# Four moves in program order in a fused transformer and expert kernel: DMA issue order, a GpSimd step, an activation table load and three VectorE instructions

## The reference

```
x = x + attn_block(layernorm(x))       # 4 layers, each:
    h = h + attention(ln(h))           #   16 heads of 8, causal mask, relative positions
    h = h + gelu(ln(h) @ W1.T + b1) @ W2.T + b2      # 128 -> 512 -> 128
x = x + experts(layernorm(x))
    shared = silu(x @ sg.T) * (x @ su.T) @ sd.T      # hidden size 256
    scores = sigmoid(x @ router.T)                   # 16 experts in 4 groups
    # the best 2 groups by their best two biased scores, then the best 4 experts of these;
    # weights = the chosen scores over their sum
    routed = sum of weight * (silu(x @ gate) * (x @ up)) @ down   # hidden size 32 each
```

## Time and profile before

| | |
|---|---|
| time, median of 3 runs | 2348.01 us (2346.59 to 2349.03) |
| the profiled execution | 2349.03 us |
| its span, first to last instruction | 2347.0 us |
| mean granted TensorE clock | 0.992 of full speed |
| PE busy | 2273.5 us, 97% |
| PE weight loads busy | 1971.6 us, 84% |
| DVE busy | 1995.8 us, 85% |
| ACT busy | 1838.7 us, 78% |
| POOL busy | 1142.6 us, 49% |

### The profile page before, as it was taken

The page is one execution under the profiler, slowest core; times in us unless marked ns, Lnnn a source line. Parts: engine busy times, 40 slices in busy tenths (PEclk is TensorE's granted clock), DMA queues, the critical chain, the costliest instruction groups (busy, mean ns, idle before and its releaser), DMA issues. The chain is left out here.

```text
span 2347.0 us, 83100 instructions
## 1 busy us (share of the span) xinstructions
PE 2273.5 (97%) x31360; PEld 1971.6 (84%) x31360; DVE 1995.8 (85%) x4943; ACT 1838.7 (78%) x2869; POOL 1142.6 (49%) x2089
## 2 busy tenths in 40 slices
PE   4999999999999999999999999999999999799999
PEld 3788888888888888888888888888888888678787
DVE  6899999988888888888888888888888887577775
ACT  2688888888888888888888888888888888655564
POOL 4555555555545554545554455554455544333332
PEclk8999999999999999999999999999999999899999
DMA  4444433333333333333333333333333332011100
GB/s 136 111 117 108 111 94 88 88 92 87 94 92 94 85 90 91 94 93 86 87 90 96 94 90 86 91 87 94 93 103 90 89 92 61 21 28 28 28 24 19
DMA packets 227431, 196.04 MB, mean 84 GB/s; under 512 B 29024, under 2 KB 225760, under 8 KB 227040
## 3 DMA queue, kind: packets, MB, share of 16 engines
q1 hardware_dynamic: 227040, 190.73, 30.2%
HBM read 14.46 MB, written 4.19 MB: 8 GB/s over the span
## 5 line engine op out<-in xcount | busy, mean ns | idle before, releaser
L995 DVE TENSOR_REDUCE rowmax<-bank 128x4 f32<-128x1024 f32 (+1 forms) x768 | 916.1, 1220 | 106.4 <-PE bank L572 73.9
L813 ACT ACTIVATE probs<-bank 128x1024 f32<-128x1024 f32 x768 | 737.7, 1024 | 82.3 <-PE bank L632 81.8
L632 PE MATMUL bank<-qstack,kstack 64*128 64x128 f32 (+1 forms) x4096 | 422.8, 299 | 4.2 <-DMA qstack<-maxrows 4.2
L572 PE MATMUL bank<-kstack,qstack 62*128 62x256 f32 (+1 forms) x4096 | 416.3, 300 | 9.5 <-DMA qstack<-base 9.5
L854 ACT ACT_TABLE_LOAD x256 | 328.4, 1283 | 4.5
L572 PEld LDWEIGHTS bank<-kstack,qstack 62*128 62x128 f32 x4096 | 315.7, 192 | 9.9 <-issue 9.9
L632 PEld LDWEIGHTS bank<-qstack,kstack 64*128 64x128 f32 x4096 | 315.1, 191 | 5.4 <-DMA qstack<-maxrows 5.4
L1169 POOL CAST xn1T_parts<-xn1T 128x256 fp32r<-128x256 f32 x128 | 50.7, 396 | 481.4 <-ACT xn1T L821 481.4
L594 PE MATMUL bank<-maskT_half,pick_half 64*128 64x128 bf16 (+1 forms) x3072 | 267.8, 241 | 10.9 <-DVE turn_c L964 2.6
L721 PE MATMUL bank<-w,hidden 128*128 128x128 f32 x2048 | 271.4, 276 | 2.7 <-ACT hidden L863 2.7
L652 PE MATMUL bank<-probs,v_pad 128*32 128x256 f32 x4096 | 271.1, 382 | 0.6 <-DVE v_tok L976 0.6
(11 more groups left out here) (153 smaller groups left out, 5187.4 us busy)
## 6 DMA issues: line engine op xcount, KB each, us to landing
qstack<-base SPq DMA_DIRECT2D x768, 128.0 KB, 2.5
kstack<-base SPq DMA_DIRECT2D x384, 128.0 KB, 2.5
turn_x<-turn_c SPq DMA_DIRECT2D x512, 32.0 KB, 1.9
qstack<-maxrows SPq DMA_DIRECT2D x256, 16.0 KB
out<-ot SPq DMA_DIRECT2D x16, 256.0 KB, 2.4
h_all<-in_x SPq DMA_DIRECT2D x7, 512.0 KB, 4.1
xin<-in_x SPq DMA_DIRECT2D x14, 256.0 KB, 3.2
w<-in_w SPq DMA_DIRECT2D x8, 256.0 KB, 3.1
```

The lines of the kernel that those rows point to most:

```text
L572: last = pe.matmul(bank[:, b0 + b, i * wide:(i + 1) * wide], qstack[rows, r, p0 + i, t * 128:(t + 1) * 128], kstack[rows, r, p0 + i, 0:wid ...
L632: last = pe.matmul(bank[:, b0 + b, i * wide:(i + 1) * wide], kstack[rows, r, p0 + i, kt * 128:(kt + 1) * 128], qstack[rows, r, p0 + i, q0: ...
L813: act.activation(probs[:, k], bank[:, A_BANK[k]:A_BANK[k] + 2, :], ACT.Exp, scale=SCALE).then_inc(exp_done[k], 1)
L995: dve.tensor_reduce(rowmax[:, n % 2, t, :, p0:p0 + heads], bank[:, M_BANK[k]:M_BANK[k] + 2, :].rearrange("p b (h c) -> p b h c", h=heads), ...
```

## The change

Four pieces of code are put elsewhere in their engine's program. No instruction is added or taken away.

- SP, layers: `content` of an item is issued at the head of the next slot, and so behind `exchange` of the same item and in front of its `turned_content`.
- POOL, layers: `turned(s)` is done at the end of slot s, behind `xn1_split(s+1)`, in place of in slot s+1 behind `xn2_split`. `split_qkv` then comes behind it.
- ACT, experts: the load of the Silu table comes directly behind the sigmoid, in front of the second `half_out`.
- DVE, experts: `weights_of_experts` is joined to the end of `routing_experts`, and so comes at u == 0 in place of u == 1 behind `result`.

```diff
@@ SP, layers
             for s in SLOTS:
                 if live(s - 1):
+                    content(s - 1)
+                if live(s - 1):
                     turned_content(s - 1)
                 if live(s - 3):
                     maxima(s - 3)
-                if live(s):
-                    content(s)
                 if live(s):
                     exchange(s)
@@ POOL, layers
                 if live(s - 6):
                     xn2_split(s - 6)
-                if live(s - 1):
-                    turned(s - 1)
...
                 if live(s + 1):
                     xn1_split(s + 1)
+                if live(s):
+                    turned(s)
@@ ACT, experts
                         act.activation(score[:].rearrange("p t e -> p (t e)"), bank[:, 6, 0:GT * E], ACT.Sigmoid
                                        ).then_inc(score_ready, 1)
+                        load_table(2 * (q + 1) + 1, ACT.Silu)
...
                     if live_tile(n - 2):
                         half_out(n - 2, 1)
-                    if u == 1 and live(q + 1):
-                        load_table(2 * (q + 1) + 1, ACT.Silu)
@@ DVE, experts
                 assert step[0] == ROUTE, step[0]
-
-            def weights_of_experts(q, v):
                 dve.tensor_scalar(wsum1[:], wsum[:], 1e-20, None, ALU.add).then_inc(route_end, 1)
...
-                    if u == 1 and live(q):
-                        weights_of_experts(q, v)
```

## The result

| | before | after |
|---|---|---|
| median (lowest to highest, runs) | 2347.66 us (2346.59 to 2349.03, 4) | 2381.52 us (2377.61 to 2389.59, 4) |
| ratio, 95% interval | | 1.0150 (1.0126 to 1.0175) |
| the profiled execution, its span | 2349.03, 2347.0 us | 2385.99, 2384.0 us |
| mean granted TensorE clock | 0.992 | 0.989 |

The forecast was 2360.2 us with a range to 2367. The profiled executions are 37.0 us apart, the medians 33.9.

A forecast was written before the change was run, and what follows sets the result against it. PE was taken to bound layers and experts, with a DMA chain pacing the first slots. Terms +5.7 - 4.2 - 2.2 + 12.9 = +12.2 us gave 2361.2 profiled, 2360.2 us against the median, range 2350 to 2367.

The forecast's parts named there:

- The sign: Whole kernel: the change makes it 0.5% slower; slower was given a chance of 0.86.
- the table load: Experts, ACT at u == 1: copy of hT and down product start 0.92 us later, 14 times, +12.9 us.
- A third sentence: Layers and experts: every engine other than PE has hundreds of microseconds free in both.
- The one-off loads: Layers, SP: loads behind an exchange, half a microsecond of issue each, fit into content's 2.9 us of cover; no cost.
- weights_of_experts: Experts, DVE: three small instructions moved before result(n-3) are hidden in 1.02 us of DVE idle time; 0 us.
- The six waits of the up product: Layers, slots with weight splits: PE waits for xn2_split behind turned, 3 x 0.58 + 3 x 1.33 = +5.7 us.
- The maxima: Layers, SP: maxima comes earlier, so PE's six waits for it go, -4.2 us, with 0 as other end.
- The first slots: Start of the layers: earlier exchange and turned_content(0) shorten PE's wait, -2.2 us, bounded by 0 and 6.7 us gained.
- The layers' three terms together: Layers: up product waits +5.7, maxima -4.2 and first slots -2.2 leave -0.7 us.
- rivals of a hidden: Experts: down does not wait for the later copy, experts cost 0, total 2347.3 us; chance 0.06.
- dearer switch: Experts: ACT empties itself before the table load, 17.9 us more, total 2378 us; chance 0.01.
- The cover of turn_x: Layers: turn_x lands 3.3 us, in some slots 1.4 us, before POOL ends xn1_split, so turned does not block POOL.

The follow-up runs named there:

- e10: The whole change, with the one-off loads issued from ACT's DMA queue in place of SP's; 2365.16 us, ratio 1.0077 against the kernel before.
- e4: Kernel before with only weights_of_experts moved, and POOL's exT_parts subtraction put behind its hw product; 2347.26 us against 2348.44, ratio 0.9994.
- e3: Kernel before with only weights_of_experts moved to the end of routing_experts; 2355.71 us, ratio 1.0028.
- e2: Kernel before with only the Silu table load moved directly behind the sigmoid; 2361.45 us, ratio 1.0056.
- e6: Kernel before with only POOL's turned moved to the end of its slot, exchange still behind content; 2423.96 us, ratio 1.0327.
- e12: The whole change, with the one-off loads issued by ACT one step later in its program, beside content; 2368.53 us against 2348.49 for the kernel before.

## Why the prediction was wrong

The sign, the table load and most of the layers' steps were right. Two steps were wrong, and both are sentences that put a cost at nothing. A third sentence is wrong without a part in the sum: the other engines do not have hundreds of microseconds free in the experts. DVE has 81 of 287 there and ACT 125.

**The one-off loads: the step that failed.** "The one-off loads behind an exchange, half a microsecond of issue each, fit into the same cover." I counted only the time in which SP issues them. But they are up to 512 KB each, and content now goes out while they move. It landed 5.4 and 7.6 us after its last issue where the prediction had 2.0, with 2.9 us of cover. The cost is the difference between the whole change and e10, where the same loads leave some 4 us ahead of content: 2381.5 - 2365.2 = 16.3 us. In the traces it is 13.8 us at the start (104.20 - 90.36), the slower clock behind the waits included, and 4.6 in slots 8 to 17 and 113: 18.4 in all, since the profiled execution of the changed kernel lies 4.5 us above its median.

**weights_of_experts: 0 in place of 7.1 us.** "DVE idles 1.02 us there for PE's down product, which hides them." The three instructions are as short as that on DVE alone (0.17, 0.18 and 0.22 us in e4). At their new place POOL's subtraction runs, and it stretches one of them from 0.17 to 1.12 us, which uses up the cover. e3 shows the cost, e4 that it goes when POOL is elsewhere.

**What held.**

- The six waits of the up product: 5.7 us forecast, 5.8 found in the lengths of the slots.
- The maxima: the wait is gone, as the 4.2 us had it. The slots that were longer before give back 3.0 us between f2(6) and f2(127), the rest lies in the start.
- The first slots: -2.2 us forecast. The times of the first round came within 0.4 us, and without loads beside content (e10) the start gained 4.4 us against the kernel before, slots 2 to 5 and their maxima included. Against e2, e3 and e4, with the same layers as before, it is 6.3 to 9.3, so the way is sure and the size is not.
- The layers' three terms together: -0.7 us forecast, and in e10, where the loads don't disturb them, -1.65 by f2(127) and -1.4 where the experts begin. The medians agree: 17.9 us for e10, less 12.4 and 7.1 for the experts, is -1.6. That near -0.7 is partly luck, since both the gain at the start and the six waits against it are several microseconds.
- The table load: 0.92 us a group forecast, 0.885 found, so the rivals of a hidden and of a dearer switch fall. The 1.28 us of the load are also what the Trainium skill gives (ScalarE: Activation LUTs, What ACT_TABLE_LOAD costs); the drain that it adds is not in these traces.
- The cover of turn_x held in the whole change, which is why turned did not make ordinary slots longer. e6 shows how near it was.

The sum made good: 12.2 + 16.3 + 7.1 = 35.6, less 0.5 for the table load and 0.7 for the layers' terms = 34.4 us, against 33.9 between the medians. That these agree to half a microsecond is luck in part: the interval of the ratio reaches from 30 to 41 us.

What stays open is whether the order in SP's queue adds something on top. In slots 8 and 14 it did not (2.08 against 2.15, 1.45 against 1.49), but in slots 11 and 17 the wait was half a microsecond longer behind the load, and in slot 5, with three loads, the wait was 7.71 us behind them and 3.17 beside them in e12, where the loads also left a little sooner against content. And since e12 can't put loads beside content in slots 2 and 3, where most of the loss arose, that they work there in the same way is inferred. And what share of the start's loss is the clock's is open, as said.

## What to carry to other kernels

When a DMA is moved, count the landing time of everything that will move at the same time, from any queue, and not the issue time: the page gives both. When a small DVE instruction is moved, look at what POOL does at the new place and not only at whether DVE is idle there. And read two moves on two engines as one if one of them relies on the other: here the POOL move alone cost 76.9 us and together with the SP move nothing in ordinary slots.

## What the runs showed of the hardware

- A DVE tensor_scalar on 128 x 4 values took 0.16 to 0.17 us alone and 1.10 to 1.13 us beside a POOL tensor_tensor on 128 x 512, ending within 0.03 us of it, in two kernels (14 groups in each).
- Six DMAs of 128 KB landed 1.9 to 2.1 us after their last issue with no load near (slot 1, to the start of the ACT instruction that waited), and 5.4 to 7.6 us after it behind loads. Beside one 512 KB load from ACT's queue it was 5.9 us: another queue gave no way round.
- Where PE stood still for DMAs at the start, slower products followed: granted clock 0.73 from 40 to 100 us in place of 0.83, and 0.50 from 94 to 100 us behind a wait of 4.12 us.
